# Five buffers for token rows, asked for four pairs ahead, and each raw weight matrix reloaded behind its own split

## The reference

```python
xn = _layernorm(x, axis=-1)
s = attn_ref(xn, ...)             # gated recurrence with 8 states, projections 256x264 and 264x256
# ffn: 32 experts, each token goes to 4 of them, cap = 1280 rows per expert
w, idx = _gate(xf, wg)
xe = xp[buf_tok].reshape(E, cap, DIM)
h = silu(einsum('ecd,edh->ech', xe, w1)) * einsum('ecd,edh->ech', xe, w3)
out = einsum('ech,ehd->ecd', h, w2) * buf_w
y = zeros.at[buf_tok].add(out)
z = silu(xf @ sw1) * (xf @ sw3) @ sw2
g = silu(y + z)
return x + s * g
```

## Time and profile before

| What | Value |
| --- | --- |
| median of 3 runs | 1176.87 us (1171.95 to 1177.72) |
| the profiled execution: span from first to last instruction | 1340.9 us |
| the profiled execution's own time | only its span is given |
| busy in it: PE, PE weight loads | 1029.3 us (77%), 984.9 us (73%) |
| busy in it: VectorE, POOL, ScalarE | 815.9 us (61%), 731.0 us (55%), 593.5 us (44%) |
| bytes moved by DMA | 183.97 MB, mean 137 GB/s |

### The profile page before, as it was taken

One profiled execution on the slowest core, in us unless ns is written; L12 is line 12 of the kernel. 1 busy time (PEld: TensorE's weight loads), 2 busy tenths in 40 slices (PEclk: granted clock), 3 DMA queues, 4 the chain that ended last, 5 costly groups with the idle time before them and its releaser, 6 DMA issues.

```text
span 1340.9 us, 30454 instructions
## 1 busy us (share of the span) xinstructions
PE 1029.3 (77%) x7933; PEld 984.9 (73%) x7933; DVE 815.9 (61%) x2705; ACT 593.5 (44%) x1314; POOL 731.0 (55%) x590
## 2 busy tenths in 40 slices
PE   6866666665666565079999999999999999999900
PEld 4865665555555564079999999999999999999900
DVE  5654555444544453256767777777767777677657
ACT  4754554444545452034444444444444444444323
POOL 1044455435444555635766666666566666665652
PEclk9977777677767776589999999999999999999955
DMA  9022222222222222366867768777786877877678
GB/s 292 33 92 92 89 90 91 91 74 91 82 91 87 100 92 101 127 158 143 176 136 169 156 138 178 153 149 167 152 181 140 175 158 152 177 159 147 96 231 284
DMA packets 157575, 183.97 MB, mean 137 GB/s; under 512 B 19242, under 2 KB 147283, under 8 KB 157523
## 3 DMA queue, kind: packets, MB, share of 16 engines
q0 software_dynamic: 55904, 79.89, 29.3%
q1 hardware_dynamic: 100992, 103.50, 25.6%
q10 hardware_dynamic: 626, 0.01, 0.0%
HBM read 85.63 MB, written 101.35 MB: 139 GB/s over the span
## 4 chain that ended last, share of the span: by engine, by line
PE 47%; another core or an unknown queue 11%; issue 11%; DMA 10%; ACT 8%; DVE 7%; SPq 4%; DVEq 1%; ACTq 0%; POOL 0%; POOLq 0%
PE h L618 9%; PE h L620 8%; PE h L619 8%; DMA rows<-slot_rows 7%; PE yb L636 4%; PE yb L638 4%; PE yb L637 4%; PE xt L602 4%; SPq L393 2%; DMA rows<-y_sum 1%; DMA out<-rows 1%; ACT acth L857 1%; ACT L828 1%; DVE w_hl L1056 1%
## 5 line engine op out<-in xcount | busy, mean ns | idle before, releaser
L618 PE MATMUL h<-xh,w_hl 128*128 (+1 forms) x1392 | 415.9, 299 | 23.7 <-issue 20.8
L619 PE MATMUL h<-xh,w_hl 128*128 (+1 forms) x1392 | 401.5, 288 | 29.1 <-issue 29.1
L620 PE MATMUL h<-xl,w_hl 128*128 (+1 forms) x1392 | 403.4, 290 | 19.4 <-issue 19.3
L517 POOL DMA_INDIRECT slot_rows<-rows,dest_idx x256 | 255.2, 997 | 292.7 <-DVE dest_idx L1209 201.4
L534 POOL DMA_INDIRECT y_sum<-rows,y_idx x156 | 247.0, 1583 | 106.7 <-DVE rows L1314 74.9
L620 PEld LDWEIGHTS h<-xl,w_hl 128*128 128x128 f32 x1392 | 272.1, 195 | 30.0 <-issue 30.0
L619 PEld LDWEIGHTS h<-xh,w_hl 128*128 128x128 f32 x1392 | 272.0, 195 | 28.6 <-issue 28.6
L618 PEld LDWEIGHTS h<-xh,w_hl 128*128 128x128 f32 x1392 | 271.5, 195 | 23.8 <-issue 23.0
L534 POOL DMA_INDIRECT y_sum<-yw,y_idx x128 | 200.9, 1570 | 157.4 <-DMA y_sum<-rows,y_idx 60.1
L857 ACT ACTIVATE acth<-act 128x256 fp32r<-128x256 f32 x348 | 126.1, 409 | 313.0 <-PE yb L638 282.5
L1091 DVE TENSOR_TENSOR actl<-act,acth 128x256 fp32r<-128x256 f32 x348 | 132.1, 421 | 148.6 <-ACT acth L857 122.1
(11 more groups left out here) (174 smaller groups left out, 1419.8 us busy)
## 6 DMA issues: line engine op xcount, KB each, us to landing
rows<-slot_rows SPq DMA_DIRECT2D x143, 289.0 KB
raw<-L_ffn_w SPq DMA_DIRECT2D x96, 256.0 KB
slot_rows<-rows SPq DMA_DIRECT2D x32, 289.0 KB
x_all<-L_attn_x SPq DMA_DIRECT2D x16, 512.0 KB, 6.0
y_sum<-yw SPq DMA_DIRECT2D x32, 256.0 KB
rows<-y_sum POOLq DMA_DIRECT2D x32, 256.0 KB, 5.1
out<-rows SPq DMA_DIRECT2D x32, 256.0 KB, 4.8
slot_rows<-rows,dest_idx POOLq DMA_INDIRECT x256
```

The costliest lines, as they stand in the source:

```text
L517: ins = pool.indirect_dma_start(slot_rows, bass.IndirectOffsetOnAxis(dest_idx[slot][:, t, k:k + 1], 0), rows[slot][:, t, :], None, bounds_ ...
L618: mm(out, high, xh[:, k, cols], start=(k == 0), stop=False)
L619: mm(out, low, xh[:, k, cols], start=False, stop=False)
L620: ins = mm(out, high, xl[:, k, cols], start=False, stop=(k == KD - 1))
```

## The change

Five buffers take the rows: pairs 1, 2 and 3 of an expert have one each (0, 1, 2), buffer 3 takes the fifth pair, or pair 0 of the next expert, and buffer 4 takes pair 0 of the next expert behind a fifth. The two new ones lie in halves of `rows` that the expert phase left unused. The first four loads are issued at once; after that a load goes out when the pair four before it has been transposed and its meta taken (`taken`, `transposed` are now raised before the wait). Each raw matrix has its own semaphore; matrix n of expert e+2 is loaded when matrix n of expert e+1 has been split, in slot n of expert e. The store of zeros for expert e+2 follows the first of them.

```diff
-        row_in = [rows[0][:, 0:2, :], rows[0][:, 2:4, :], rows[2][:, 0:2, :]]
+        row_in = [rows[0][:, 0:2, :], rows[0][:, 2:4, :], rows[2][:, 0:2, :], rows[2][:, 2:4, :], rows[1][:, 2:4, :]]
...
-        raw_loaded = sem("raw_loaded")
+        raw_loaded = [sem(f"raw_loaded{n}") for n in range(3)]
...
-        row_loaded = [sem(f"row_loaded{n}") for n in range(3)]
+        row_loaded = [sem(f"row_loaded{n}") for n in range(len(row_in))]
...
-        def row_buffer(slot):
-
-            return 2 if slot == PAIRS else slot % 2
-
-        def row_fills(e, slot):
-
-            return 2 * e + slot // 2 + 1 + slot % 2
+        def next_fills(e, slot):
+
+            return e + 1 + (slot == PAIRS - 1)
...
-            def load_raw(e):
-                for n, w in enumerate((w1, w3, w2)):
-                    sp.dma_start(raw_view(n),
-                                 w[bass.ds(e, 1), :, :].rearrange("a (k p) n -> p (a k) n", p=P)
-                                 ).then_inc(raw_loaded, 16)
+            def load_raw(e, n):
+                sp.wait_ge(wh_ready, 3 * e + 1 + n)
+                sp.wait_ge(wl_ready, 3 * e + 1 + n)
+                sp.dma_start(raw_view(n), (w1, w3, w2)[n][bass.ds(e, 1), :, :].rearrange("a (k p) n -> p (a k) n", p=P)
+                             ).then_inc(raw_loaded[n], 16)
...
-            load_raw(0)
+            for n in range(3):
...
-            def load_rows(e, j, buf, started=2, zeros_too=False):
-
-
-                before_last, before_last_xt, stored = sp.snap(taken), sp.snap(transposed), sp.snap(zeros)
+            def load_rows(e, j, buf, free=True, zeros_too=False):
+
+                if free:
+                    sp.reg_add(taken, taken, 1)
+                    sp.reg_add(transposed, transposed, 1)
+                this_taken, this_transposed, stored = sp.snap(taken), sp.snap(transposed), sp.snap(zeros)
                 if zeros_too:
                     sp.wait_ge(zeros_stored, stored)
-                if started >= 2:
-                    sp.wait_ge(xt_ready, before_last_xt)
-                    sp.wait_ge(meta_taken, before_last)
+                if free:
+                    sp.wait_ge(xt_ready, this_transposed)
+                    sp.wait_ge(meta_taken, this_taken)
                 sp.dma_start(row_in[buf], slot_rows[bass.ds(e * STRIDE + j * PAIR, PAIR), :]
                              .rearrange("(t p) c -> p t c", p=P)).then_inc(row_loaded[buf], 16)
-                if started:
-                    sp.reg_add(taken, taken, 1)
-                    sp.reg_add(transposed, transposed, 1)
-
-            def section(e, first, last):
+
+            def section(e, ahead):
 
                 fifth = sp.value_load(has_fifth[0:1, bass.ds(e, 1)], min_val=0, max_val=1)
-                load_rows(e, 1, row_buffer(0), 1 if first else 2)
-                if not last:
-                    sp.wait_ge(wh_ready, e * 3 + 6)
-                    sp.wait_ge(wl_ready, e * 3 + 6)
-                    load_raw(e + 1)
-                    store_zeros(e + 1)
-                load_rows(e, 2, row_buffer(1))
-                load_rows(e, 3, row_buffer(2))
-
-                def next_first(slot):
-                    if last:
-                        load_rows(0, 0, row_buffer(slot))
+
+                def next_first(buf):
+                    if ahead:
+                        load_rows(e + 1, 0, buf, zeros_too=True)
                     else:
-                        load_rows(e + 1, 0, row_buffer(slot), zeros_too=True)
+                        load_rows(0, 0, buf)
 
                 with sp.If(fifth > 0):
-                    load_rows(e, 4, row_buffer(3))
-                    next_first(4)
+                    load_rows(e, PAIRS, PAIRS - 1)
+                    next_first(PAIRS)
                 with sp.If(fifth < 1):
-                    next_first(3)
-
-            load_rows(0, 0, 1, 0, zeros_too=True)
-            section(0, True, False)
-            with sp.Fori(1, E - 1) as e:
-                section(e, False, False)
-            section(E - 1, False, True)
-            sp.reg_add(taken, taken, 1)
-            sp.reg_add(transposed, transposed, 1)
+                    next_first(PAIRS - 1)
+                if ahead:
+                    for n in range(3):
+                        if ahead > 1:
+                            load_raw(e + 2, n)
+                            if n == 0:
+                                store_zeros(e + 2)
+                        load_rows(e + 1, n + 1, n)
+
+            load_rows(0, 0, PAIRS - 1, False, zeros_too=True)
+            for n in range(3):
+                load_rows(0, n + 1, n, False)
+            for n in range(3):
+                load_raw(1, n)
+            store_zeros(1)
+            with sp.Fori(0, E - 2) as e:
+                section(e, 2)
+            section(E - 2, 1)
+            section(E - 1, 0)
+            for _ in range(PAIRS):
+                sp.reg_add(taken, taken, 1)
+                sp.reg_add(transposed, transposed, 1)
             taken_all, transposed_all = sp.snap(taken), sp.snap(transposed)
             sp.wait_ge(xt_ready, transposed_all)
             sp.wait_ge(meta_taken, taken_all)
...
-            look_ahead(0, 1, 1)
+            look_ahead(0, PAIRS - 1, 1)
...
-                    fills = count.fifths_now() + 1 if slot == PAIRS else row_fills(e, slot)
+                    fills = count.fifths_now() + 1 if slot == PAIRS else next_fills(e, slot)
                     up(q + A_PAIRS, w_hl[w_slot], bass.ds((q % 2) * PAIR, PAIR),
-                       lambda: look_ahead(q + 1, row_buffer(slot), fills))
+                       lambda: look_ahead(q + 1, slot, fills))
...
             def split_high(wts, loads, matrices=range(3)):
-                sc.wait_ge(raw_loaded, loads)
                 for n in matrices:
+                    sc.wait_ge(raw_loaded[n], loads)
                     av(wts[:, 2 * n, :, :], raw_view(n), ACT.Copy).then_inc(wh_ready, 1)
...
-                        split_high(w_hl[1 - w_slot], e * 48 + 144, (slot,))
+                        split_high(w_hl[1 - w_slot], e * 16 + 48, (slot,))
...
-                    take_meta(q + 1, row_buffer(slot), fifths + 1 if slot == PAIRS else row_fills(e, slot))
+                    take_meta(q + 1, slot, fifths + 1 if slot == PAIRS else next_fills(e, slot))
```

More of the change, by code:

```diff
@@ L381, in _ @@
             for n, w in enumerate((sw1, sw3, sw2)):
-                sp.dma_start(raw_view(n), weight_view(w)).then_inc(raw_loaded, 16)
+                sp.dma_start(raw_view(n), weight_view(w)).then_inc(raw_loaded[n], 16)
             for g in range(2, GROUPS):
@@ L414, in _ @@
             sp.wait_ge(dispatch_ready, GROUPS)
-            load_raw(0)
+            for n in range(3):
+                load_raw(0, n)
             sp.wait_ge(counts_ready, 1)
@@ L886, in _ @@
             xhigh(0, region(0))
-            split_high(w_hl[1], 48)
+            split_high(w_hl[1], 16)
             sc.wait_ge(setup_dve, SETUP_DVE)
@@ L921, in _ @@
             take_z(A_PAIRS - 1)
-            split_high(w_hl[0], 96)
+            split_high(w_hl[0], 32)
             av(warm[:, :], iota_f[0:1, 0:1], ACT.Silu)
@@ L1318, in _ @@
             v.memset(pad[:, :], 0.0).then_inc(y_ready, 2)
-            take_meta(0, 1, 1)
+            take_meta(0, PAIRS - 1, 1)
             xlow(A_PAIRS, region(0), (h3_ready, A_PAIRS - 1))
```

## The result

| Kernel | Median | Runs |
| --- | --- | --- |
| before | 1175.34 us | 1171.95 to 1177.72 |
| changed | 1212.01 us | 1208.51 to 1214.55 |

A forecast was written before the change was run, and what follows sets the result against it. PE was taken to bound the expert phase at 4.70 us a pair. Removing 18 row stalls (20.7 us) and their restarts (4.0) gave 24.7 us, all other terms 0: 1176.87 - 24.7 = 1152.2 us, range 1139 to 1170.

The forecast's parts named there:

- PE as the bound, 4.70 us a pair: Expert phase: PE's 40 matmuls a pair take 4.70 us, and nothing that leaves them alone can be faster.
- All 18 row stalls go: PE's transposes: row loads four pairs ahead remove 20.7 us of waits and 4.0 us of restarts, together 24.7 us.
- Raw loads and waits on SP priced at 0: SP's order: raw loads behind their own splits and three waits an expert gain and lose nothing, 0 us.
- start of the phase at 0: Start of the expert phase: four row loads at once, then raw, cost 0, at worst 3.4 us.
- What is late next: POOL's scatter-adds: 16.6 of 18.8 us a four-pair expert, 2.2 us to spare, so 4.3 us idle at the boundary is free.
- The store of zeros: Slot 0, in an 834 KB burst beside POOL's drain: at worst 4.0 us idle there, which costs nothing.
- The same drain, slower than before: Rival, expert boundary: the burst lengthens POOL's drain to 6.3 us idle, 24 us slower, 1201 us; chance 0.04.
- POOL's drain takes back part: Rival, expert boundary: with 5.0 us idle POOL sets the pace in 18 experts, 12.6 us, giving 1165 us; chance 0.12.
- Stalls smaller when nothing is recorded: Rival, PE's row waits: they are shorter in an unrecorded execution, giving 1163 to 1170 us; chance 0.10.

The follow-up runs named there:

- the second trace: The kernel before, unchanged, traced again: 1168.09 us in one run, with a first phase of 402 us and an expert phase of 693 us.
- The block in slot 3: The changed kernel with its three raw loads and the zeros in one block behind the third split: 1167.77 us, 0.9945 of before.
- the split loads with the zeros late: The changed kernel with the store of zeros behind the third raw load in place of the first: 1166.88 us, 0.9954 of before.
- the cut raw load: The changed kernel with only 8 of 128 partitions of the first raw matrix loaded in the loop: 1.030 of before.
- the best version: Five row buffers, raw loads and zeros in a block in slot 3, one more y buffer for slot 3: 1161.65 us, 0.988 of before.
- the zeros in slot 3: The changed kernel with the zeros behind the row load of pair 3, on a slower chip: 1344.79 us, 0.998 of before.

## Why the prediction was wrong

- *PE as the bound, 4.70 us a pair.* Right. Between stalls PE's transposes come 4.71 us apart in the kernel before and in the changed one.
- *All 18 row stalls go.* Right: PE waits for no row load after 450 us. The size, 24.7 us, was that of the shown trace; in the second one the 17 waits sum to 16.2 us, with 17 x 0.22 for the restarts 20 us. That this much becomes gain failed with the step below.
- *Raw loads and waits on SP priced at 0; start of the phase at 0.* These held as far as the runs show. The block in slot 3 and the split loads with the zeros late give the same time (1167.77 and 1166.88 us), and the cut raw load changed nothing beside the store. One more load of 256 KB in slot 0, without the store there, did cost 0.8%. That the lead of four pairs carries the waits for the splits is shown by the 1436 us that they cost without it.
- *What is late next.* **This step failed.** I compared POOL's work in an expert, 16.6 us, with PE's 18.8, and took the 2.2 us between them as free at the boundary, 4.3 us idle in all. POOL's rate is not what binds. The adds of slot 1 must land before VectorE writes slot 3's y into `yw`. The second timeline above gives the true cover: from 518.19, when slot 1's first tile lies in `yw`, to 527.1 are 8.9 us. The two adds need 1.85 + 5.3 = 7.15 (the second is issued at 523.82 and lands at about 529.1). That leaves 1.8 us for POOL to begin after y is there, and it begins after 3.8. (Some 0.8 of either is the usual hand-over from VectorE to POOL: in slot 3 y is in `yw` at 529.93, and POOL begins at 530.73.) The 2.0 missing are the 2.20 that VectorE waits. With a fourth buffer, and the drain as late, the same SP order is 0.994 of before.
- *The store of zeros.* I moved it in the sum as part of a burst of 834 KB, and set its price by bytes. Its price is that of a store to HBM beside adds that are waited for. In the kernel before it was issued 10 us ahead of the boundary's drain (at 518.33, against a drain from 528.49, in the second trace).
- *The rivals.* "The same drain, slower than before" named the mechanism's first half and the right sign, but set its point of decision at 5.5 us idle, and gave it 0.04. The measured mean is 4.2 us, below even the 4.3 that I called free, so no count by POOL's rate could have found this loss. "POOL's drain takes back part" had 4.0 us idle as the worst and free; the mean passed it. "The same drain, slower than before" also let 18 experts pay 2.0 and 13 pay 1.0. In fact 28 of the 31 boundaries stalled, and two pairs just before one, together by 64.4 us more than 30 x 4.71 between transposes, or 2.1 each. Of this the waits of PE for y are 45.3 us (28 times), and some 7.5 are the stretches at the lower clock, for which I had no term. 64.4 less the 20.5 us that the 18 longer transposes of the second trace of before sum to, counted in the same way, are 43.9, the 43 us of the windows.
- *Stalls smaller when nothing is recorded.* The excess of the shown trace was all in its first phase, and no part of this.

## What to carry to other kernels

When a wait for the landing of DMAs stands in the program, look at what other queues issue just before it: a small store to HBM there cost more than three times what a larger load did (3.2% against 0.8%). The cover of a late step is not the engine's free time in a period but the distance to the next reuse of a buffer, measured in the timeline from the write into it to the next write. And a stall that is removed may have given slack to others: of some 20 us of row stalls, 12 to 14 us became gain even in the best version.

## What the runs showed of the hardware

A store of 144 KB to HBM in another queue lengthened the wait for scatter-adds to land from 3.1 to 4.0 us, one of 289 KB to 4.2 and two of them to 5.1, while 256 KB loaded from HBM or copied within SBUF gave 3.5 and 3.7. TensorE's granted clock fell from 1.00 to 0.50 behind PE's five longest waits in the changed kernel (2.08 to 2.71 us) and behind none of up to 1.87.

The shown trace of the kernel before took 572 us for the first phase, at a mean granted clock of 0.76, and the second 402 at 0.87; the expert phases, near full clock, were 692 and 693 us. It seems to be a matter of the chip: on one, seven runs of the kernel before took 1338.76 to 1352.17 us, and the trace of the zeros in slot 3 has 0.77 in its first 572 us; on the others it took 1170 to 1187.
